# Moving a small transposition behind the convolution, in a TensorE-bound attention and feed-forward kernel

## The chip, the cores and the metric

The kernel runs on one core of one Trainium2 chip. The metric is the device time of one execution in microseconds, taken as the median of several runs. Engines are called by the profile's names: PE (TensorE, with PEld for its weight loads), DVE (VectorE), ACT (ScalarE), POOL (GpSimd), SP (SyncE, which issues most DMAs).

## The reference

The input x is 128 x 32 x 512. Cut to what matters here, the reference computes this:

```python
# per batch element: rows are mixed with weights that depend on cond
y  = einsum('boi,bih->boh', agg_w(cond), x) + agg_b(cond)
# attention: 32 query heads, 8 key/value heads, head size 16, rope, causal
x  = x + softmax(causal(q(y) @ k(y).T / 4)) @ v(y) @ Wo
# grouped convolution with 9 taps, plus a term of cond
z  = conv(x, weight, groups=4, taps=9) + ctx(cond) + bias
# feed-forward: a base product plus a low-rank part with routed experts
h  = z @ A.T                         # 8 experts x rank 16 = 128 columns
w  = routed expert weights from softmax(z @ router_W.T)
x  = x + z @ base_W.T + base_b + ((h * w) @ B) * 2
```

The kernel calls `h * w` **hw**. It is 128 tokens x 128, and has to be transposed before it can be multiplied by B ("lora").

## The kernel before, in words

**Tiling.** The 128 batch elements are taken in 32 groups (G = 32) of four, so that one group has 128 tokens and fills the 128 partitions. Products need more precision than one pass gives, so each operand is split into a high part (`_hi`, a rounded copy) and a low part (`_lo`, the value minus its high part), and a product is three matmuls: high x high, high x low, low x high.

**Software pipeline.** All engines run the same hand-written loop over t, each with its own `steps(t)`, and meet only through semaphores. Step t does the attention of group t, the projection of y into queries, keys and values for group t+1, the convolution of group t-1, and the feed-forward and lora of group t-2. Steps -1 to 3 and 31 to 33 are unrolled; steps 4 to 30 are 27 turns of a hardware loop, in which the count in a wait comes from a register. The order inside a step is that of the code, engine by engine.

**The part of PE's step that matters.** After the projection of group t+1 (L420), PE transposes the normalized softmax of group t (`transpose_p`, L642, eight matmuls into banks 2 and 4), then hw of group t-2 (`transpose_hw`, L669, into bank 7), then runs the convolution (`conv`, L623: four matmuls with 96 rows and 32 columns each, each in its own column group and recorded as two passes), then the attention's values (`values`, L662: 16 matmuls of 64 rows and 32 columns, recorded as 32 passes, into banks 4 and 7), then `lora` (L561 into bank 6, L564 into bank 2), then the output projection (`project`, L576, twelve matmuls into bank 3). In the loop, `values` first issues a tiny matmul with two columns that nobody reads (L656); it carries the last of the waits that stand ahead of the values: `vB_in` (the values' DMA), `hwT_lo_sb` (bank 7 has been read) and `pT_sb` (the transposed softmax has been copied).

**ACT.** Its step copies the first half of the transposed softmax (`transposed_p(t, 0)`), then hwT into `hwT_hi`, then the second half, then half of the attention's output into `oT_hi`, then the values of the next group into `vS` (all these copies are recorded at L755).

**DVE.** After the routing of group t-2, which ends with hw (L1130), it does the rope of the next group's queries (L1141, L1143), then `hwT_lo` (the `minus` helper, L980), then the rope of the keys (L1141, L1143 again, smaller), then `low_oT`: the other half of `oT_hi` (L1190) and `oT_lo` (L980), then the bias of the convolution (L1199) and the two output additions (L1209, L1211). `project` waits for both halves of `oT_hi`.

**DMA.** SP loads the convolution's input `xc` (recorded as scratch, L385) and the values `vB` (L355) early in each step.

Of the kernel before, what the change touches and what calls it, by code (L numbers as in the profile page):

```python
# [15 lines left out]
P = 128  # L16
B = 128
S = 32
D = 512
NB = P // S  # L20
G = B // NB
# [15 lines left out]
BASE6 = 2 * P  # L37
# [33 lines left out]
def live(u):  # L71

    return not isinstance(u, int) or 0 <= u < G


def peeled(t, n):

    return isinstance(t, int) and t == n
# [8 lines left out]
def build(nc, x, cond, fside, cW0, cb0, cW1, cb1, cW2, cb2, cweight, cbias, Wq, Wk, Wv, Wo,  # L87
          convw, convc, baseW, baseb, routerW, routerb, loraA, loraB, emap, const, out):
    with ExitStack() as ctx:
# [321 lines left out]
        def _(pe):  # L411
# [143 lines left out]
            def lora(u):  # L555

                pe.wait_ge(hwT_hi_sb, u + 1)
                pe.wait_ge(hwT_lo_sb, u + 1)
                terms = ((hwT_hi, lora_hi), (hwT_hi, lora_lo), (hwT_lo, lora_hi))
                for n, (a, b) in enumerate(terms):  # L560
                    last = mm(ps[:, 6, 0:BASE6], a[:, :], b[:, 0:BASE6], start=False, stop=(n == 2))  # L561
                last.then_inc(ffn_ps, 1)
                for n, (a, b) in enumerate(terms):
                    last = mm(ps[:, 2, 0:D - BASE6], a[:, :], b[:, BASE6:D], start=(n == 0), stop=(n == 2))  # L564
                last.then_inc(last_ps, 1)

            def project(u):

# [75 lines left out]
                    if b % 2:  # L644
                        last.then_inc(pT_ps, 1)

            def values(t):

                pe.wait_ge(vB_in, 16 * HK * (t + 1))
                if live(t - 2):  # L650
                    pe.wait_ge(hwT_lo_sb, t - 1)
                if peeled(t, 1):
                    pe.wait_ge(base_lo_sb, PH)
                pe.wait_ge(pT_sb, 2 * t + 2)
                if not isinstance(t, int):
                    mm(ps[0:S, 4, 0:2], convW[:, 0, :, :].rearrange("p j o -> p (j o)"), xc[:, 0, 0:2], start=True, stop=True)  # L656
                for b in range(NB):
                    for h in range(2):
                        for r in range(2):
                            rows = slice(2 * S * r, 2 * S * (r + 1))  # L660
                            to = S * (2 * h + (r + b) % 2)
                            last = mm(ps[to:to + S, 4 + 3 * (b % 2), b // 2 * P:(b // 2 + 1) * P],  # L662
                                      vB[rows, b, h, :], prT[rows, 2 * b + h, :], start=True, stop=True)
                last.then_inc(o_ps, 1)

            def transpose_hw(u):

                pe.wait_ge(hw_sb, u + 1)
                nc.tensor.transpose(ps[:, 7, 0:P], hw[:, :, :].rearrange("p e r -> p (e r)"), ident).then_inc(hwT_ps, 1)  # L669

            def steps(t):
                if peeled(t, 1):
                    pe.wait_ge(base_lo_sb, 2)
                if live(t):
                    transpose_qk(t)
                if peeled(t, 0):
                    prepare_ar()
                if peeled(t, 2):
                    pe.wait_ge(base_lo_sb, PH)
                if live(t - 2):  # L680
                    transpose_z(t - 2)
                if peeled(t, G + 1):
                    keep_warm(3)
                if peeled(t, -1):
                    pe.wait_ge(mixw0_sb, 1)
                if peeled(t, 3):
                    pe.wait_ge(mixw_in, 16 * NB)
                if peeled(t, 0):
                    pe.wait_ge(mixw_in2, 16 * NB)
                if live(t + 1):  # L690
                    mix(t + 1)
                if peeled(t, -1):
                    first_bias()
                    mixing_weights()
                if peeled(t, 2):
                    prepare_lora()
                if live(t):
                    scores(t)

                if peeled(t, 1):  # L700
                    prepare_base((2, 3))
                if live(t - 2):
                    feed_forward(t - 2)
                if live(t + 1):
                    queries(t + 1)
                    keys_values(t + 1)

                if peeled(t, -1):
                    prepare_conv()
                if peeled(t, 0):  # L710
                    pe.wait_ge(convW_sb, 1)
                if live(t):
                    transpose_p(t)
                if peeled(t, 0):
                    pe.wait_ge(prep_sb, 1)
                    prepare_base((0, 1))
                if peeled(t, G - 1):
                    conv(t - 1)
                if peeled(t, G):
                    pe.wait_ge(sx_sb, 2 * G)  # L720
                    keep_warm(4)
                if live(t - 2):
                    transpose_hw(t - 2)
                if peeled(t, G) or peeled(t, G + 1):
                    keep_warm(3)
                if peeled(t, G):
                    lora(t - 2)
                if live(t - 1) and not peeled(t, G - 1):
                    conv(t - 1)
                if peeled(t, G):  # L730
                    keep_warm(2)
                if live(t):
                    values(t)
                if live(t - 2) and not peeled(t, G):
                    lora(t - 2)
                if peeled(t, 0):
                    pe.wait_ge(wo_hi_sb, NQ)
                    pe.wait_ge(wo_lo_sb, NQ)
                if live(t):
                    project(t)  # L740
# [4 lines left out]
        def _(act):  # L745
# [8 lines left out]
            def copy(dst, src):  # L754
                return nc.scalar.activation(dst, src, ACT.Copy)  # L755
# [85 lines left out]
            def steps(t):  # L841
                if live(t):
                    act.wait_ge(qT_ps, t + 1)
                    copy(qT, ps[:, 4, :].rearrange("p (g b q) -> p b g q", g=NQ, b=NB)).then_inc(qT_sb, 1)
                if live(t - 2):
                    act.wait_ge(zT_ps, t - 1)
                    copy(z_hi[:, :, :].rearrange("p j (q o) -> p j q o", o=CG), z_transposed()).then_inc(z_hi_sb, 1)
                if peeled(t, 0):
                    act.wait_ge(rope_t, 2)
                    keep_values()  # L850
                    prepare_ar()
                if live(t + 1):
                    next_y_hi(t + 1)
                if peeled(t, 0):
                    prepare_wo((0, 1))
                if peeled(t, -1):
                    prepare_kv()
                    keep_mixing_weights()
                if peeled(t, 2):
                    prepare_lora()  # L860
                if live(t):
                    exponentials(t, 0)
                if live(t - 2):
                    act.wait_ge(ar_ps, t - 1)
                    copy(arS[:, :], ps[:, 7, D - BASE6:D - BASE6 + NAR]).then_inc(ar_sb, 1)
                if live(t):
                    exponentials(t, 1)
                if live(t - 2):
                    act.wait_ge(top_sb, t - 1)
                    nc.scalar.activation(ex[:, :], lg[:, :], ACT.Exp, bias=top[:, :], accum_out=exZ[:, :]).then_inc(ex_sb, 1)  # L870
                if peeled(t, 0):
                    prepare_wo((2, 3))
                if peeled(t, 1):
                    prepare_base((2, 3))

                if live(t):
                    transposed_p(t, 0)
                if live(t) and peeled(t, G - 1):
                    transposed_p(t, 1)
                if live(t - 2):  # L880
                    act.wait_ge(hwT_ps, t - 1)
                    copy(hwT_hi[:, :], ps[:, 7, 0:P]).then_inc(hwT_hi_sb, 1)
                if live(t) and not peeled(t, G - 1):
                    transposed_p(t, 1)
                if live(t):
                    act.wait_ge(o_ps, t + 1)
                    copy(heads(oT_hi, 0), heads_ps(0)).then_inc(oT_hi_sb, 1)
                if peeled(t, 0):
                    prepare_base((0, 1))
                if live(t + 1) and not peeled(t, -1):  # L890
                    act.wait_ge(rope_t, 2 * (t + 2))
                    keep_values()
# [82 lines left out]
        def _(dve):  # L975
# [237 lines left out]
            def steps(t):  # L1213
# [47 lines left out]
                    prepare_conv()  # L1261
                if live(t - 2):
                    dve.wait_ge(hwT_hi_sb, t - 1)
                    minus(hwT_lo[:, :], ps[:, 7, 0:P], hwT_hi[:, :]).then_inc(hwT_lo_sb, 1)
                if live(t + 1) and not peeled(t, -1):
                    rope(t + 1, 1, qkv_ps, D, P)
                if live(t):
# [35 lines left out]
```

## Time and profile before

| | us |
|---|---|
| median of 3 runs | 617.46 |
| the three runs | 617.46, 617.57, 613.9 |
| the profiled execution, own time | 615.38 |
| its span, first to last instruction | 613.6 |
| PE busy | 585.4 (95% of the span) |
| PEld busy | 492.8 (80%) |
| DVE busy | 494.0 (81%) |
| ACT busy | 221.4 (36%) |
| POOL busy | 226.7 (37%) |

The mean granted clock of TensorE is 0.997 of full speed. The hardware turns of the loop are alike and follow each other every 17.53 us. The profile is read in four ways here: the page's share of the chain that ended last; that chain in order of time; the timeline of single turns, whose rows give start, duration, engine, line, operation and what ended the idle time before; and the waits summed by line.

### The profile page before, as it was taken

The numbers are of one execution on the slowest core, as the hardware profiler recorded it, in microseconds if no ns is written. First come the engines' busy times: TensorE is split into PE (matmuls) and PEld (weight loads), VectorE is DVE, ScalarE is ACT, GpSimd is POOL, SyncE is SP. The second block draws the span as 40 slices with busy tenths as digits, with TensorE's granted clock in tenths as the row PEclk, the third lists the DMA queues.
The fourth block names the chain that finished last, engine by engine and source line by source line (L and its number), as shares of the span: only waits on it lengthen the run. The fifth ranks groups of instructions, "written<-read, shape, count | busy, mean of one in ns | idle before, by whom it ended". The sixth has DMA issues, their size and how long they took to land.

```text
span 613.6 us, 14243 instructions
## 1 busy us (share of the span) xinstructions
PE 585.4 (95%) x4928; PEld 492.8 (80%) x4928; DVE 494.0 (81%) x1236; ACT 221.4 (36%) x603; POOL 226.7 (37%) x182
## 2 busy tenths in 40 slices
PE   4988999999999999999999999999999999999875
PEld 4666798888888988888889888888898878888664
DVE  4677888888888888888888888888888878888843
ACT  4263334333333333333333333333333333333311
POOL 8164234433333344333333443333334333343310
PEclk9989999999999999999999999999999999999999
DMA  7844454344545543445555434454554344554430
GB/s 195 174 115 114 112 134 127 100 101 106 118 116 133 133 121 98 104 106 118 116 133 133 121 99 104 105 118 116 133 133 121 88 107 104 111 133 111 112 86 36
DMA packets 125206, 71.26 MB, mean 116 GB/s; under 512 B 48781, under 2 KB 107309, under 8 KB 125064
## 3 DMA queue, kind: packets, MB, share of 16 engines
q1 hardware_dynamic: 123696, 70.53, 48.0%
q10 hardware_dynamic: 1352, 0.27, 0.3%
q0 software_dynamic: 144, 0.28, 0.2%
q8 instruction: 8, 0.13, 0.1%
q14 instruction: 6, 0.05, 0.0%
HBM read 51.53 MB, written 19.53 MB: 116 GB/s over the span
## 4 chain that ended last, share of the span: by engine, by line
PE 83%; DVE 6%; DMA 5%; issue 2%; ACT 1%; SPq 1%; ACTq 1%; DVEq 0%
PE ps L420 19%; PE ps L576 15%; PE ps L597 10%; PE ps L603 6%; PE ps L623 5%; DMA scratch<-x_dram 5%; PE ps L524 4%; PE ps L615 4%; PE ps L642 4%; PE ps L662 3%; PE ps L561 3%; PE ps L587 2%; PE ps L631 2%; PE ps L564 2%; PE ps L611 1%
## 5 line engine op out<-in xcount | busy, mean ns | idle before, releaser
L957 POOL TENSOR_TENSOR qk<-network,t 128x640 f32<-128x640 f32 x31 | 48.3, 1560 | 161.2 <-DVE t L1143 161.2
L420 PE MATMUL ps<-wqkv_hi,y_hi 128*128 128x512 f32 (+1 forms) x256 | 88.2, 345 | 3.6 <-DVE raw L1162 2.2
L420 PE MATMUL ps<-wqkv_hi,y_lo 128*128 128x512 f32 (+1 forms) x256 | 88.3, 345 | 0.0
L420 PE MATMUL ps<-wqkv_lo,y_hi 128*128 128x512 f32 (+1 forms) x256 | 88.1, 344 | 0.0
L969 POOL TENSOR_TENSOR raw<-x1p,basebB 128x512 f32<-128x512 f32 x32 | 49.5, 1548 | 58.2 <-DVE x1p L1222 58.2
L755 ACT ACTIVATE raw<-ps 128x512 f32<-128x512 f32 x64 | 37.8, 595 | 74.3 <-PE ps L642 74.2
L964 POOL TENSOR_TENSOR raw<-raw,zero 128x512 f32<-128x512 f32 x32 | 33.3, 1041 | 72.1 <-DVE raw L1211 72.1
L420 PEld LDWEIGHTS ps<-wqkv_hi,y_hi 128*128 128x128 f32 x256 | 49.3, 192 | 11.8 <-DVE raw L1162 3.6
L941 POOL TENSOR_TENSOR raw<-raw,rz 128x512 f32<-128x512 f32 x32 | 33.7, 1052 | 56.4 <-DVE rz L1172 56.4
L420 PEld LDWEIGHTS ps<-wqkv_lo,y_hi 128*128 128x128 f32 x256 | 49.3, 193 | 6.2
L420 PEld LDWEIGHTS ps<-wqkv_hi,y_lo 128*128 128x128 f32 x256 | 49.1, 192 | 6.0
L817 ACT ACTIVATE raw<-raw 128x512 f32<-128x512 f32 x64 | 40.4, 632 | 34.0 <-DVE raw L1162 31.1
L755 ACT ACTIVATE qk_t<-ps 128x512 f32<-128x512 f32 x32 | 19.1, 597 | 91.6 <-PE ps L587 91.6
L597 PE MATMUL ps<-ffn_hi,z_hi 128*128 128x400 f32 x128 | 46.9, 366 | 2.3 <-DVE z_lo L980 2.3
L947 POOL TENSOR_TENSOR y_lo<-ys,y_hi 128x512 fp32r<-128x512 f32 x31 | 40.4, 1305 | 21.0 <-ACT y_hi L755 21.0
L1151 DVE TENSOR_TENSOR qk_t<-ps,cst 128x512 f32<-128x512 f32 x32 | 22.1, 691 | 32.2 <-PE ps L585 32.1
L1160 DVE TENSOR_REDUCE mx<-ps 128x16 f32<-128x512 f32 x64 | 43.9, 686 | 2.7 <-PE ps L615 0.4
L1162 DVE TENSOR_TENSOR raw<-ps,mx 128x512 f32<-128x512 f32 x64 | 44.3, 692 | 2.2
L597 PE MATMUL ps<-ffn_lo,z_hi 128*128 128x400 f32 x128 | 44.4, 346 | 0.0
L597 PE MATMUL ps<-ffn_hi,z_lo 128*128 128x400 f32 x128 | 44.0, 344 | 0.0
L1170 DVE TENSOR_REDUCE sm<-raw 128x16 f32<-128x512 f32 x64 | 41.8, 653 | 0.0
L755 ACT ACTIVATE vS<-ps 32x64 f32<-32x64 f32 (+1 forms) x192 | 37.5, 226 | 1.1
(185 smaller groups left out, 1459.9 us busy)
## 6 DMA issues: line engine op xcount, KB each, us to landing
scratch<-x_dram SPq DMA_DIRECT2D x96, 256.0 KB, 5.8
x_dram<-x1p SPq DMA_DIRECT2D x32, 260.0 KB, 2.1
xm<-x SPq DMA_DIRECT2D x32, 256.0 KB, 4.4
xr<-x SPq DMA_DIRECT2D x32, 256.0 KB, 2.7
out<-raw SPq DMA_DIRECT2D x32, 256.0 KB, 2.0
v_dram<-vS SPq DMA_DIRECT2D x32, 64.0 KB
vB<-v_dram SPq DMA_DIRECT2D x128, 16.0 KB, 4.9
mixb<-mixb_dram SPq DMA_DIRECT2D x28, 64.0 KB, 3.8
```

The lines of the kernel that those rows point to most:

```text
L420: last = mm(dst, a, b, start=(n == 0), stop=(n == 3 * len(left) - 1))
L576: last = mm(ps[:, 3, :], a[:, g, :, :].rearrange("p b q -> p (b q)"), b[:, g, :], start=(n == 0 and g == 0), stop=(n == 2 and g == NQ - 1))
L597: last = mm(ps[:, 7, 0:D - BASE6 + NAR], a, b[:, BASE6:D + NAR], start=(n == 0), stop=(n == len(terms) - 1))
L603: mm(ps[:, 6, 0:BASE6], a, b[:, 0:BASE6], start=(n == 0), stop=False)
L755: return nc.scalar.activation(dst, src, ACT.Copy)
L817: nc.scalar.activation(pr[:, D * h:D * (h + 1)], sx[:, D * h:D * (h + 1)], ACT.Exp, scale=HD ** -0.5).then_inc(p_sb, 1)
L947: nc.gpsimd.tensor_tensor(y_lo[:, :], ys[:, :], y_hi[:, :].bitcast(F32), ALU.subtract).then_inc(y_lo_sb, 1)
L957: nc.gpsimd.tensor_tensor(qk[:, :], t1, t2[:, :], ALU.add).then_inc(qk_sb, 1)
L969: nc.gpsimd.tensor_tensor(x1c, x1, basebB[:, :].rearrange("p (n j) -> p j n", j=PH), ALU.add).then_inc(x1c_sb, 1)
L1160: v.tensor_reduce(m, s3, AX.X, ALU.max).then_inc(mx_sb, 1)
L1162: v.tensor_tensor(sx[:, D * h:D * h + D].rearrange("p (h m) -> p h m", m=S), s3, m.unsqueeze(2).broadcast_to([P, 16, S]), ALU.subtract).th ...
L1170: v.tensor_reduce(sm[:, m], p3, AX.X, ALU.add).then_inc(sm_sb, 1)
```

## The change

On PE, the transposition of hw moves from ahead of the convolution to behind it, and writes bank 3 instead of bank 7. The waits that stood ahead of the values, without that for `hwT_lo_sb`, now stand ahead of this transposition (`values_ready`), and the unread product is gone. In `lora`, the four matmuls with `hwT_hi` come first, and the wait for `hwT_lo_sb` stands ahead of the last two. On ACT, both halves of the transposed softmax are copied ahead of `hwT_hi`. On DVE only the bank that is read changes. Steps 31 to 33 keep their order, since the convolution was ahead of the transposition in step 31 already, and step 32 keeps its transposition and lora ahead of the convolution; they take over the new waits and the new order inside `lora`.

```diff
             def lora(u):
                 pe.wait_ge(hwT_hi_sb, u + 1)
+                for n, right in enumerate((lora_hi, lora_lo)):
+                    mm(ps[:, 6, 0:BASE6], hwT_hi[:, :], right[:, 0:BASE6], start=False, stop=False)
+                for n, right in enumerate((lora_hi, lora_lo)):
+                    mm(ps[:, 2, 0:D - BASE6], hwT_hi[:, :], right[:, BASE6:D], start=(n == 0), stop=False)
                 pe.wait_ge(hwT_lo_sb, u + 1)
-                terms = ((hwT_hi, lora_hi), (hwT_hi, lora_lo), (hwT_lo, lora_hi))
-                for n, (a, b) in enumerate(terms):
-                    last = mm(ps[:, 6, 0:BASE6], a[:, :], b[:, 0:BASE6], start=False, stop=(n == 2))
-                last.then_inc(ffn_ps, 1)
-                for n, (a, b) in enumerate(terms):
-                    last = mm(ps[:, 2, 0:D - BASE6], a[:, :], b[:, BASE6:D], start=(n == 0), stop=(n == 2))
-                last.then_inc(last_ps, 1)
+                mm(ps[:, 6, 0:BASE6], hwT_lo[:, :], lora_hi[:, 0:BASE6], start=False, stop=True).then_inc(ffn_ps, 1)
+                mm(ps[:, 2, 0:D - BASE6], hwT_lo[:, :], lora_hi[:, BASE6:D], start=False, stop=True).then_inc(last_ps, 1)
...
-            def values(t):
+            def values_ready(t):
                 pe.wait_ge(vB_in, 16 * HK * (t + 1))
-                if live(t - 2):
-                    pe.wait_ge(hwT_lo_sb, t - 1)
                 if peeled(t, 1):
                     pe.wait_ge(base_lo_sb, PH)
                 pe.wait_ge(pT_sb, 2 * t + 2)
-                if not isinstance(t, int):
-                    mm(ps[0:S, 4, 0:2], convW[:, 0, :, :].rearrange("p j o -> p (j o)"), xc[:, 0, 0:2], start=True, stop=True)
+
+            def values(t):
+                if not live(t - 2):
+                    values_ready(t)
...
             def transpose_hw(u):
                 pe.wait_ge(hw_sb, u + 1)
-                nc.tensor.transpose(ps[:, 7, 0:P], hw[:, :, :].rearrange("p e r -> p (e r)"), ident).then_inc(hwT_ps, 1)
+                if live(u + 2):
+                    values_ready(u + 2)
+                nc.tensor.transpose(ps[:, 3, 0:P], hw[:, :, :].rearrange("p e r -> p (e r)"), ident).then_inc(hwT_ps, 1)
...
-                if peeled(t, G - 1):
-                    conv(t - 1)
                 if peeled(t, G):
                     pe.wait_ge(sx_sb, 2 * G)
                     keep_warm(4)
-                if live(t - 2):
                     transpose_hw(t - 2)
-                if peeled(t, G) or peeled(t, G + 1):
                     keep_warm(3)
-                if peeled(t, G):
                     lora(t - 2)
-                if live(t - 1) and not peeled(t, G - 1):
+                if live(t - 1):
                     conv(t - 1)
+                if live(t - 2) and not peeled(t, G):
+                    transpose_hw(t - 2)
+                if peeled(t, G + 1):
+                    keep_warm(3)
...
                 if live(t):
                     transposed_p(t, 0)
-                if live(t) and peeled(t, G - 1):
                     transposed_p(t, 1)
                 if live(t - 2):
                     act.wait_ge(hwT_ps, t - 1)
-                    copy(hwT_hi[:, :], ps[:, 7, 0:P]).then_inc(hwT_hi_sb, 1)
-                if live(t) and not peeled(t, G - 1):
-                    transposed_p(t, 1)
+                    copy(hwT_hi[:, :], ps[:, 3, 0:P]).then_inc(hwT_hi_sb, 1)
...
                     dve.wait_ge(hwT_hi_sb, t - 1)
-                    minus(hwT_lo[:, :], ps[:, 7, 0:P], hwT_hi[:, :]).then_inc(hwT_lo_sb, 1)
+                    minus(hwT_lo[:, :], ps[:, 3, 0:P], hwT_hi[:, :]).then_inc(hwT_lo_sb, 1)
```

On PE, in the body of the loop, this is the order before, from the transposed softmax (`ps<-cst,raw`) over hw, the convolution (`scratch,convW`), the unread product (32x2) and the values (`raw,vB`) to lora:

```order
L642 MATMUL ps<-cst,raw 128x128 x7
L669 MATMUL ps<-cst,hw 128x128 [waits hw_sb]
L621 REGISTER_ALU
L623 MATMUL ps<-scratch,convW 32x512 [waits xc_in]
L623 MATMUL ps<-scratch,convW 32x512 x3
L649 REGISTER_ALU
L654 REGISTER_ALU [waits hwT_lo_sb,vB_in]
L656 MATMUL ps<-scratch,convW 32x2 [waits pT_sb]
L662 MATMUL ps<-raw,vB 32x128 x16
L561 MATMUL ps<-lora_hi,hwT_hi 128x256 [waits hwT_lo_sb,hwT_hi_sb]
L561 MATMUL ps<-lora_lo,hwT_hi 128x256
L561 MATMUL ps<-lora_hi,hwT_lo 128x256
```

And this is the same place after the change:

```order
L641 MATMUL ps<-cst,raw 128x128 x7
L620 REGISTER_ALU
L622 MATMUL ps<-scratch,convW 32x512 [waits xc_in]
L622 MATMUL ps<-scratch,convW 32x512 x3
L648 REGISTER_ALU [waits hw_sb]
L651 REGISTER_ALU [waits vB_in]
L671 MATMUL ps<-cst,hw 128x128 [waits pT_sb]
L662 MATMUL ps<-raw,vB 32x128 x16
L559 MATMUL ps<-lora_hi,hwT_hi 128x256 [waits hwT_hi_sb]
L559 MATMUL ps<-lora_lo,hwT_hi 128x256
L561 MATMUL ps<-lora_hi,hwT_hi 128x256
L561 MATMUL ps<-lora_lo,hwT_hi 128x256
```

The transposition of hw has taken the place of the unread product, and the values wait for nothing of their own.

On DVE the order is the same in both kernels. This is its part of the loop from hw to the output's first addition, of the kernel before (`network` and `t` are the rope's two buffers):

```order
L1130 SCALAR_TENSOR_TENSOR hw<-arS,exR,we 128x128 [waits we_sb]
L1141 TENSOR_TENSOR network<-ps,cst 128x512 [waits qk_sb,q_ps]
L1143 TENSOR_TENSOR t<-ps,cst 128x32x8 x2
L980 TENSOR_TENSOR hwT_lo<-ps,hwT_hi 128x128 [waits hwT_hi_sb]
L1141 TENSOR_TENSOR network<-ps,cst 128x128 [waits qk_sb,qkv_ps]
L1143 TENSOR_TENSOR t<-ps,cst 128x8x8 x2
L1190 CAST oT_hi<-ps 128x8x32 [waits o_ps]
L980 TENSOR_TENSOR oT_lo<-ps,oT_hi 128x8x32 [waits oT_hi_sb]
```

Nothing moved here: the wait for `hwT_hi_sb` still stands ahead of the rope of the keys and of `oT_hi`.

## Rows read from the trace of the kernel before

**Rows 1.** The page: busy times, and the chain that ended last by engine

```profile
PE 585.4 (95%) x4928; PEld 492.8 (80%) x4928; DVE 494.0 (81%) x1236; ACT 221.4 (36%) x603; POOL 226.7 (37%) x182
...
PE 83%; DVE 6%; DMA 5%; issue 2%; ACT 1%; SPq 1%; ACTq 1%; DVEq 0%
```

**Rows 2.** The chain in order of time, one turn: start, us, what

```profile
302.46 0.11 PE ps L669
302.57 1.00 PE ps L623 x8
303.57 0.16 PE ps L656 x2
```

**Rows 3.** Timeline of one turn of the loop, PE: start, us, engine, line, operation

```profile
302.30 0.27 PE L669 MATMUL ps<-cst,hw 128*128 128x128 f32 x1
302.50 0.16 PEld L623 LDWEIGHTS ps<-scratch,convW 96*32 96x32 f32 x8 [0.17 <-DMA scratch<-x_dram]
...
303.50 0.14 PEld L656 LDWEIGHTS ps<-scratch,convW 96*32 96x32 f32 x2 [0.85 <-ACT raw L755]
...
303.66 0.67 PE L662 MATMUL ps<-raw,vB 64*32 64x128 f32 x32
...
304.26 0.39 PE L561 MATMUL ps<-lora_hi,hwT_hi 128*128 128x256 f32 x1
...
305.06 1.10 PE L576 MATMUL ps<-wo_hi,oT_hi 128*128 128x512 f32 x4
```

**Rows 4.** Timeline of the same turn, ACT and DVE

```profile
302.61 0.28 ACT L755 ACTIVATE hwT_hi<-ps 128x128 fp32r<-128x128 f32 x1
302.78 0.59 ACT L755 ACTIVATE raw<-ps 128x512 f32<-128x512 f32 x1
302.99 0.28 DVE L980 TENSOR_TENSOR hwT_lo<-ps,hwT_hi 128x128 fp32r<-128x128 f32 x1
...
303.38 0.35 DVE L1143 TENSOR_TENSOR t<-ps,cst 128x64 f32<-128x64 f32 x2
...
304.43 0.42 DVE L1190 CAST oT_hi<-ps 128x256 fp32r<-128x256 f32 x1 [0.70 <-PE ps L662]
```

**Rows 5.** Timeline, two turns in which the convolution's input came late

```profile
250.01 0.16 PEld L623 LDWEIGHTS ps<-scratch,convW 96*32 96x32 f32 x8 [0.28 <-DMA scratch<-x_dram]
...
496.40 0.16 PEld L623 LDWEIGHTS ps<-scratch,convW 96*32 96x32 f32 x8 [1.20 <-DMA scratch<-x_dram]
...
497.20 0.20 PEld L656 LDWEIGHTS ps<-scratch,convW 96*32 96x32 f32 x2 [0.64 <-issue]
497.42 0.40 PEld L662 LDWEIGHTS ps<-raw,vB 64*32 64x32 f32 x32
```

**Rows 6.** Timeline of step 31, where hw is already transposed behind the convolution

```profile
583.24 0.33 PE L669 MATMUL ps<-cst,hw 128*128 128x128 f32 x1
583.61 0.28 ACT L755 ACTIVATE hwT_hi<-ps 128x128 fp32r<-128x128 f32 x1 [1.41 <-PE ps L669]
583.92 0.29 DVE L980 TENSOR_TENSOR hwT_lo<-ps,hwT_hi 128x128 fp32r<-128x128 f32 x1 [0.73 <-ACT hwT_hi L755]
584.28 0.43 PEld L662 LDWEIGHTS ps<-raw,vB 64*32 64x32 f32 x32 [0.90 <-issue]
...
585.73 1.09 PE L576 MATMUL ps<-wo_hi,oT_hi 128*128 128x512 f32 x4
```

**Rows 7.** Timeline of step 32, from the convolution to a full-array product

```profile
598.44 0.16 PEld L623 LDWEIGHTS ps<-scratch,convW 96*32 96x32 f32 x8
...
599.44 0.30 PEld L468 LDWEIGHTS ps<-wo_hi 128*128 128x128 f32 x2 [0.84 <-issue]
```

**Rows 8.** Timeline of step 2: hw, the convolution, and the output projection

```profile
74.32 0.14 PEld L669 LDWEIGHTS ps<-cst,hw 128*128 128x128 f32 x1 [0.89 <-DVE hw L1130]
...
74.58 0.16 PEld L623 LDWEIGHTS ps<-scratch,convW 96*32 96x32 f32 x8
...
77.26 1.09 PE L576 MATMUL ps<-wo_hi,oT_hi 128*128 128x512 f32 x4
```

## The prediction

> **What bounds the kernel now.** I read the page first. PE is busy for 95% of the span, and the chain that ended last lies on PE for 83% [rows 1]. Then I read that chain in order of time: inside the loop it never leaves PE. One turn goes from hw's transposition (0.11 us) and the convolution (1.00) straight to the unread product (0.16) [rows 2], and from there over the values (303.66 to 304.26) into lora [rows 3]. So whatever shortens PE's row by a tenth of a microsecond in each of the 27 turns gives 2.7 us, and whatever makes PE wait costs as much. Third, the timeline of one turn shows what PE waits for at the place of the change. The weights of the unread product were loaded at 303.50, after ACT's second softmax copy had ended at 302.78 + 0.59 = 303.37 [rows 3, 4]: 0.13 from ACT's end to PE's start. The convolution, which began at 302.50, was over at that moment too, so PE hardly stood still. The output projection started at 305.06, right behind lora; its other input, DVE's half of oT_hi, was ready at 304.43 + 0.42 = 304.85 [rows 3, 4]. So DVE had only 0.21 us in hand. That is the number to watch.
>
> **The convolution moves forward.** In that turn hw's transposition began at 302.30 and the convolution at 302.50 [rows 3]: 0.20 from a full-array product to the convolution. hw's own share of PE's row was 0.11 [rows 2], so with hw gone from this place the convolution starts at about 302.39, if its input is there. In 21 of the 27 turns the input did not delay it; in six it did, by a few hundredths to one microsecond; two of them are shown [rows 5].
>
> **hw's transposition behind the convolution.** It uses the full array. Step 32 shows what that costs: the convolution began at 598.44 and the next full-array weights at 599.44, with nothing to wait for and 0.84 us of idle loader ahead [rows 7]. So hw's weights load 1.00 us after the convolution's start, at 303.39. The unread product had it easier: with the convolution's own shape, its weights went in 0.80 us after a late convolution's start (497.20 against 496.40), and the values followed 1.02 us after it [rows 5]. From hw's weights to the next tiled product it is 0.26 us (74.32 to 74.58) [rows 8], so the values start at 303.39 + 0.26 = 303.65, where they started at 303.66. Neither of the moved waits is late: the second softmax copy no longer has hwT_hi ahead of it, which took 302.61 to 302.78, so it ends at 303.20 and releases PE at 303.33; hw itself has been ready since before the old place. The product that goes saves 0.16, the moved one saves 0.11 at its old place and costs 0.26 at its new one: PE's own row gains 0.01.
>
> The Trainium skill (TensorEngine Tiling, Key Properties) says that a change of tiling mode, not just of tile, drains the engine. By that rule the change adds one such change per turn, full array between two tiled products, and the trace agrees with its 0.84 us of idle loader.
>
> **The new wait on DVE.** What hangs on hw now starts a microsecond later. Step 31 has this order already. There ACT's hwT_hi started 0.37 after hw's product, and DVE's hwT_lo 0.31 after that [rows 6]. From 303.39 this gives hwT_hi at 303.76 to 304.04 and hwT_lo at 304.07 to 304.36; in the turn shown hwT_lo started at 302.99 [rows 4]. DVE takes its work in order, and behind hwT_lo stand the rope of the keys and then oT_hi. The rope ended 0.74 after hwT_lo's start (303.38 + 0.35 against 302.99) [rows 4]; a DVE instruction that has nothing to wait for starts up to 0.09 before the end of the one ahead, so oT_hi starts 0.66 to 0.74 after hwT_lo. I take 0.66, since this is how the rows of the rope follow each other. So oT_hi starts at 304.73, not 304.43, and ends at 305.15. From DVE's end to PE it was 0.07 in step 31 (584.21 to 584.28) [rows 6]; the projection has one more wait, I take 0.08. It starts at 305.23, not 305.06: **0.17 us later**. Ends: 0.10 if the overlap and the release are a little better; 0.28 if the convolution's input, which is not seen to land early, never lets it start before 302.50.
>
> Lora is not the one that is late: it starts at 303.65 + 0.60 = 304.25, when hwT_hi has been there for 0.2 us, comes to its low part at about 304.84, when hwT_lo has been there for 0.5 us, and has issued its six products at 305.05. Its new order hides nothing that was open in the loop; at its old order it would have had hwT_lo in time too. Behind the waiting projection are only PE's own later products, and by the timeline DVE and POOL have room there.
>
> **The sum over the loop.** In each turn the projection now starts 1.00 + 0.37 + 0.31 + 0.66 + 0.42 + 0.08 = 2.84 us after the convolution. Before, it was 305.06 - 302.50 = 2.56. With a convolution 0.11 earlier this is +0.17, times 21 turns = +3.6. In the six turns with a late input nothing moves forward, and the slack of up to 0.15 that the short product left is lost too: +0.28 to +0.43 each, three near each end by how late they were, together +2.3. Loop: **+5.9 us**.
>
> **Outside the loop.** Step 3 had no unread product: it loses 0.17 and the 0.16 that it never spent, some 0.3. In step 2, hw came late and held the convolution: 0.89 us of idle loader ahead of hw [rows 8]. Now the convolution can start 0.17 after the softmax weights, at 73.60, and the projection 2.84 later, at 76.44, not 77.26. This is -0.82 if its input is there, and +0.16 if it comes as late as 74.58; no row tells, I take -0.6. In step 31 the values no longer wait for hwT_lo: they start 0.26 after hw, at 583.50, not 584.28, lora follows and the projection starts at 584.90, not 585.73 [rows 6]: -0.8. In steps 32 and 33 lora's high part goes ahead of the wait for hwT_lo; the last product comes 0.3 earlier in step 32, and at the very end DVE's addition waits for one product after the low part, not three: -0.05. Together -1.4.
>
> **Total:** +5.9 - 1.4 = +4.5 us, 0.7%. The profiled execution took 615.4, the median of the runs shown is 617.5. I start half way, from 616.4, and come to **620.9**.
>
> **Rivals.**
> (A) *The full-array weights slip under the convolution.* If hw's weights can be loaded while the convolution still streams, as those of the unread product were [rows 5], its product starts some 0.15 earlier and the chain over DVE with it: the projection is where it was, +0.02 a turn; the loop costs about 1, the ends give 1.4: 616.0, not slower. Against it stands the idle loader of step 32 [rows 7].
> The Trainium skill (TensorE: Matmul & The Clock Gate, Architectural detail) says that PE can pull weight loads ahead of matmuls in flight. By that rule this case would be the one; step 32 does not show it.
> (B) *PE alone decides.* If besides that DVE's chain had its slack back (the rope's rows closer than I read them), the PE row would lose 0.15 a turn: -4 in the loop, -1.4 outside: 611.0. It needs oT_hi 0.15 earlier than rows 4 and 6 give, and I see nothing for it.
> (C) *The convolution's input sets the start in every turn.* The wait ahead of the convolution is put down to this DMA even in the turn shown, where it cost nothing [rows 3]. If it lands just at the old start, moving hw away gives nothing: 21 x 0.28 + 2.3 = 8.2 in the loop, -0.6 outside: 624.0, slower. It decides once the input lands after 302.39 in this turn's time.
> (D) *DVE becomes the bound.* It is busy for 81% [rows 1] and would stand still for 1 us more per turn, but it idled 0.70 at oT_hi [rows 4] and has idle time behind it. It decides if the late hwT_lo costs DVE 0.4 us a turn or more: 10.8 - 1.4, or 626.
>
> **How the numbers follow.** My forecast 0.55, A 0.14, B 0.05, C 0.18, D 0.08. The range that holds 8 in 10 runs from 614.0 (A with its spread) to 626.0 (C, and D's edge). One percent, 6.2 us, is about what a measurement of this kernel can tell from no change. Faster by over 1%: what is in B, 0.06. Slower by over 1%: C, D and the upper edge of the forecast, 0.30. Within 1%: 0.64.
>
> **What would show it.** In the new profile: the chain in order of time leaves PE in each turn, over hwT_hi, hwT_lo and oT_hi, ahead of the projection; a wait of the projection for DVE's oT_hi (L1188 or near), 0.1 to 0.2 us in all 27 turns; hw's weights 1.00 us after the convolution's; a period of 17.7 us instead of 17.53; DVE idle ahead of hwT_lo for about 1 us. I would be wrong in the step on the drain if hw's weights load under 0.95 us after the convolution's start, in the step on DVE if the projection follows lora without a gap, and in both if the period is below 17.53.

## The result, and the profile after

| | before | after |
|---|---|---|
| median | 616.48 us (4 runs, 613.9 to 617.57) | 623.32 us (4 runs, 620.9 to 624.0) |
| ratio | | 1.0117, 95% interval 1.008 to 1.0154 |
| profiled execution, own time | 615.38 | 623.83 |
| its span | 613.6 | 622.0 |

The change made the kernel 1.2% slower. The forecast was 620.9, 0.7% slower, with a range from 614.0 to 626.0.

The page of the changed kernel shows nearly the same busy shares as [rows 1]; the share of DMA in the chain that ended last has doubled, and that of PE has fallen:

```profile
PE 592.7 (95%) x4874; PEld 491.9 (79%) x4874; DVE 491.6 (79%) x1236; ACT 225.9 (36%) x603; POOL 226.3 (36%) x182
...
PE 76%; DMA 11%; DVE 5%; SPq 3%; issue 2%; ACT 1%; ACTq 1%; DVEq 0%
```

That share is no measure of the loss: it is 10% in the rope-first run below, which is as fast as the kernel before, and 1% in the changed kernel with an earlier input, which is nearly as slow as this one.

This is the chain of the changed kernel in order of time over one turn of the loop (start, us, what), which answers to [rows 2]:

```profile
307.14 1.00 PE ps L622 x8
308.13 0.26 PE ps L671
308.39 0.60 PE ps L662 x32
308.99 0.43 PE ps L559 x2
309.42 0.24 PE ps L561 x2
309.66 0.12 PE ps L563
309.77 0.12 PE ps L564
309.89 0.03 issue
309.92 3.04 PE ps L575 x12
```

hw's transposition (L671) takes 0.26 us behind the convolution. Near the bottom there are 0.03 us of "issue": in this turn, this small row is all that the chain sets apart from PE's own work. The projection's row has 3.04 us where the kernel before and the first experiment below have 2.81, but only a part of that is slower work. In the timeline the projection takes 2.88 us from its own start to that of the next product (309.92 to 312.80), against 2.81 in both others; the other 0.16 us is waiting that the chain has booked as projection (the last product of lora starts at 309.61, and these follow each other every 0.12, so with the 0.03 the wait is 0.19). The chain names DVE nowhere in this turn: a reader who looks only for engine names there will miss the wait.

The timeline of the same turn is what [rows 3, 4] were before:

```profile
307.06 0.16 PEld L622 LDWEIGHTS ps<-scratch,convW 96*32 96x32 f32 x8 [0.17 <-DMA scratch<-x_dram]
...
308.06 0.14 PEld L671 LDWEIGHTS ps<-cst,hw 128*128 128x128 f32 x1 [0.84 <-ACT raw L756]
...
308.32 0.67 PE L662 MATMUL ps<-raw,vB 64*32 64x128 f32 x32
308.43 0.28 ACT L756 ACTIVATE hwT_hi<-ps 128x128 fp32r<-128x128 f32 x1 [0.60 <-PE ps L671]
308.74 0.29 DVE L978 TENSOR_TENSOR hwT_lo<-ps,hwT_hi 128x128 fp32r<-128x128 f32 x1 [1.00 <-ACT hwT_hi L756]
...
309.14 0.34 DVE L1141 TENSOR_TENSOR t<-ps,cst 128x64 f32<-128x64 f32 x2
...
309.40 0.41 DVE L1188 CAST oT_hi<-ps 128x256 fp32r<-128x256 f32 x1
...
309.89 0.76 PEld L575 LDWEIGHTS ps<-wo_hi,oT_hi 128*128 128x128 f32 x4 [0.20 <-issue]
309.92 1.16 PE L575 MATMUL ps<-wo_hi,oT_hi 128*128 128x512 f32 x4
```

Read from the convolution's start: hw's weights at +1.00, the values at +1.26, hwT_hi at +1.37, hwT_lo at +1.68, oT_hi at +2.34, the projection at +2.86. The projection was at +2.56 before. DVE's oT_hi has no idle time ahead of it any more, where it idled 0.70 in [rows 4]; the idle time has moved up, ahead of hwT_lo (1.00). The loader of the projection stood still for 0.20 us. The profile puts that down to "issue", because DVE's oT_hi ended only 0.08 us before (309.40 + 0.41 = 309.81); it is the wait for DVE all the same, as the first experiment shows.

One line of the waits summed by line (total us, times, longest) has all turns of it:

```profile
PEld ps L575 <- issue: 6.8, 30, 1.0
```

The regular turns follow each other every 17.78 us, not every 17.53. Eight turns of the loop had a late convolution input, with 2.9 us of idle loader beyond the usual 0.17; in the profile of before it was six turns with 1.9 us.

**Where the 8.4 us of span are.** The convolution of step 4 starts at 110.38 instead of 109.62: +0.8. From there to the one of step 30 there are 26 periods, which take 465.4 us instead of 457.3: +8.1, of which 26 x 0.25 = 6.5 is in the regular turn and 1.6 in the turns with a late input. The rest of the program is 0.5 shorter. Medians of several runs differ by less, 6.8 us. Each profile is a single execution, and executions of one kernel differ: in their late inputs, and in where the granted clock falls (the last section). How much of the gap between 8.4 and 6.8 is due to either is not shown. The clock is not the cause of the loss: the changed kernel's only execution at a mean granted clock of 1.000 took 620.9 us, and the kernel before took 613.5 to 613.7 us in its four at that clock.

### The profile page after: what moved, and what is told of

Same layout as the page of the kernel before. It is cut to its first block, busy times and chain, and to the rows that moved or that the text cites. A ratio compares the mean times of both kernels' runs of the same rounds, so it can differ in the third digit from the quotient of the medians.

```text
span 622.0 us, 14076 instructions
## 1 busy us (share of the span) xinstructions
PE 592.7 (95%) x4874; PEld 491.9 (79%) x4874; DVE 491.6 (79%) x1236; ACT 225.9 (36%) x603; POOL 226.3 (36%) x182
## 4 chain that ended last, share of the span: by engine, by line
PE 76%; DMA 11%; DVE 5%; SPq 3%; issue 2%; ACT 1%; ACTq 1%; DVEq 0%
PE ps L420 16%; PE ps L575 16%; DMA scratch<-x_dram 10%; PE ps L596 9%; PE ps L622 5%; PE ps L602 5%; PE ps L524 3%; PE ps L614 3%; PE ps L662 3%; PE ps L641 3%; PE ps L559 2%; DVE x1p L1220 2%; PE ps L586 2%; PE ps L630 2%; PE ps L671 1%
## 5 line engine op out<-in xcount | busy, mean ns | idle before, releaser
L756 ACT ACTIVATE raw<-ps 128x512 f32<-128x512 f32 x64 | 34.7, 595 | 74.2 <-PE ps L641 74.1
L575 PE MATMUL ps<-wo_hi,oT_hi 128*128 128x512 f32 x128 | 37.3, 413 | 2.2 <-DVE oT_hi L1188 0.7
```

Of the source, the lines that this page charges most:

```text
L575: last = mm(ps[:, 3, :], a[:, g, :, :].rearrange("p b q -> p (b q)"), b[:, g, :], start=(n == 0 and g == 0), stop=(n == 2 and g == NQ - 1))
```

## The experiments

All ratios are against the kernel before, run on the same chip between the others.

### The rope of the keys ahead of hwT_lo

The edit, on DVE in the changed kernel:

```diff
-                if live(t - 2):
-                    dve.wait_ge(hwT_hi_sb, t - 1)
-                    minus(hwT_lo[:, :], ps[:, 3, 0:P], hwT_hi[:, :]).then_inc(hwT_lo_sb, 1)
                 if live(t + 1) and not peeled(t, -1):
                     rope(t + 1, 1, qkv_ps, D, P)
+                if live(t - 2):
+                    dve.wait_ge(hwT_hi_sb, t - 1)
+                    minus(hwT_lo[:, :], ps[:, 3, 0:P], hwT_hi[:, :]).then_inc(hwT_lo_sb, 1)
```

> The changed kernel, but on DVE the rope of the keys stands ahead of hwT_lo, so that DVE's half of oT_hi no longer waits behind the rope behind hwT_lo. If the loss comes from that queue on DVE, the projection follows lora without a gap, 2.66 us after the convolution's start instead of 2.86, its first four matmuls take 1.10 us again instead of 1.16, the period falls from 17.78 to about 17.53, and the time to about 616.5 us. If the loss comes from the extra full-array product between two tiled ones, or from the convolution's input, nothing changes: 622 to 624 us.

Measured: 614.62 us, ratio 0.998 (0.9964 to 0.9996). The regular period is 17.53 (17.52 and 17.53 by turns). The timeline of one turn:

```profile
304.83 0.33 PE L671 MATMUL ps<-cst,hw 128*128 128x128 f32 x1
...
305.51 0.29 DVE L978 TENSOR_TENSOR hwT_lo<-ps,hwT_hi 128x128 fp32r<-128x128 f32 x1 [0.53 <-ACT hwT_hi L756]
...
305.87 0.42 DVE L1188 CAST oT_hi<-ps 128x256 fp32r<-128x256 f32 x1
...
306.50 1.09 PE L575 MATMUL ps<-wo_hi,oT_hi 128*128 128x512 f32 x4
```

oT_hi now starts 1.04 us after hw's product instead of 1.34, and the projection 1.67 after it instead of 1.86, without a gap behind lora and with 1.09 instead of 1.16 for its first four matmuls. The line "PEld ps L575 <- issue" shrank from 6.8 us in 30 turns to 1.0 us in one. hwT_lo still starts 0.68 us after hw's product, as in the changed kernel: the rope of the keys now fills time in which DVE idled. Moving these instructions on DVE took back all that the change had lost: the loss was the queue on DVE. The extra change between full array and tiles is still in this kernel and does not make it slower than before.

### The bank alone

The kernel before, with hw transposed into bank 3, where it stood, and without the values' wait for hwT_lo:

```diff
-                nc.tensor.transpose(ps[:, 7, 0:P], hw[:, :, :].rearrange("p e r -> p (e r)"), ident).then_inc(hwT_ps, 1)
+                nc.tensor.transpose(ps[:, 3, 0:P], hw[:, :, :].rearrange("p e r -> p (e r)"), ident).then_inc(hwT_ps, 1)
...
-                if live(t - 2):
-                    pe.wait_ge(hwT_lo_sb, t - 1)
```

> The kernel before with the bank alone changed: hw is transposed at its old place, but into bank 3, and the values no longer wait for hwT_lo; the unread product stays. All theories: that wait was never the last one in the loop, so the loop is as before (period 17.53); step 31 and step 2 gain up to 0.8 us each where the values did wait for it. 614.5 to 616.5 us, within 0.3% of before. If the bank itself costs something, it is slower.

Measured: 612.9 us, ratio 0.9956 (0.9932 to 0.9981): more than expected. The regular period is 17.46, not 17.53. The wait that I had called "never the last" cost 0.07 us a turn. The timeline shows where, the ends of ACT's copy and the unread product (L654 here):

```profile
300.81 0.59 ACT L753 ACTIVATE raw<-ps 128x512 f32<-128x512 f32 x1
...
301.45 0.14 PEld L654 LDWEIGHTS ps<-scratch,convW 96*32 96x32 f32 x2 [0.77 <-ACT raw L753]
```

Only 0.05 us lie between them, where [rows 3, 4] have 0.13. Two more runs went after this.

### One more wait, long satisfied

To the bank-3 kernel one wait was added, on hw:

```diff
                 pe.wait_ge(vB_in, 16 * HK * (t + 1))
+                if live(t - 2):
+                    pe.wait_ge(hw_sb, t - 1)
```

> The bank-3 run with one more wait on PE ahead of the unread product, against a register and on hw_sb, which has been satisfied long before. In the bank-3 run the period fell from 17.53 to 17.46 when the wait for hwT_lo went, though that was never the last to be satisfied. If PE's issue of a wait costs that time, the period is 17.53 again; if hwT_lo's semaphore itself did it, it stays 17.46. 612 to 616 us.

Measured: 613.47 us, ratio 0.996 (0.9939 to 0.9982), most periods 17.46. An extra wait in the same place costs nothing here; it was the wait for hwT_lo in particular.

### ACT's new order with the old bank

The kernel before with only this edit on ACT (the wait for hwT_lo ahead of the values stays):

```diff
-                if live(t) and peeled(t, G - 1):
-                    transposed_p(t, 1)
+                if live(t):
+                    transposed_p(t, 1)
                 if live(t - 2):
                     act.wait_ge(hwT_ps, t - 1)
                     copy(hwT_hi[:, :], ps[:, 7, 0:P]).then_inc(hwT_hi_sb, 1)
-                if live(t) and not peeled(t, G - 1):
-                    transposed_p(t, 1)
```

> The kernel before with only ACT's order changed: both softmax copies ahead of hwT_hi, hw still in bank 7 and the values still waiting for hwT_lo. hwT_lo then ends some 1.14 us after the convolution's start, clearly last. In the kernel before it ended 0.77 us after it, and the unread product started 0.23 us after that. If a wait for hwT_lo in the middle of the three takes 0.23 us from DVE's end to PE, the unread product's weights load 1.37 us after the convolution's start and the period is 17.90; if it takes the usual 0.07 to 0.13, 1.21 to 1.27 us and 17.74 to 17.80. 620 to 628 us either way: this is what bank 7 costs with ACT's new order.

Measured: 624.7 us in a single execution, beside 616.13 for one of the kernel before; the reading rests on the regular turns, which are alike. The timeline:

```profile
306.88 0.16 PEld L623 LDWEIGHTS ps<-scratch,convW 96*32 96x32 f32 x8 [0.17 <-issue]
...
307.73 0.29 DVE L978 TENSOR_TENSOR hwT_lo<-ps,hwT_hi 128x128 fp32r<-128x128 f32 x1 [0.27 <-ACT hwT_hi L755]
...
308.26 0.14 PEld L656 LDWEIGHTS ps<-scratch,convW 96*32 96x32 f32 x2 [1.22 <-ACT raw L755]
```

The unread product's weights load 1.38 us after the convolution's start and 0.24 after hwT_lo's end; the next convolution starts 17.91 after this one. This is the first of the two cases, to 0.01 us. The profile's own label is wrong: ACT's copy had ended 0.7 us earlier. In the kernel before, hwT_lo ended at 302.99 + 0.28 = 303.27 and the unread product came at 303.50 [rows 3, 4], the same 0.23. So hwT_lo, not ACT, released the unread product there. Why this wait, the second of three, takes 0.23 us from DVE to PE, when step 31 had 0.07 [rows 6], was not tried; the last section says what the traces add.

### Both softmax copies first, hw ahead of the convolution

The bank-3 kernel with ACT's new order (the edit above, with bank 3). The unread product stays.

> The kernel before with bank 3 (as in e3) and both softmax copies ahead of hwT_hi on ACT; hw stays ahead of the convolution, the unread product stays. The second copy ends 0.17 us earlier, so the unread product's weights load while the convolution still streams, as they did in turns with a late input, and the values start 1.01 us after the convolution, not 1.16. hwT_lo is then 0.46 us later than before and still leaves oT_hi in time. Period 17.38 instead of 17.53, time 610 to 612.5 us, 0.7% faster than before. If the unread product costs its 0.16 us wherever it stands, nothing changes: 615 to 616.5 us.

Measured: 610.26 us, ratio 0.9934 (0.9911 to 0.9956). The regular period is 17.39. The timeline of one turn:

```profile
299.53 0.16 PEld L623 LDWEIGHTS ps<-scratch,convW 96*32 96x32 f32 x8 [0.17 <-issue]
...
300.23 0.30 PEld L654 LDWEIGHTS ps<-scratch,convW 96*32 96x32 f32 x2 [0.54 <-ACT raw L753]
...
300.54 0.67 PE L660 MATMUL ps<-raw,vB 64*32 64x128 f32 x32
...
301.32 0.42 DVE L1186 CAST oT_hi<-ps 128x256 fp32r<-128x256 f32 x1 [0.18 <-PE ps L660]
...
301.95 1.09 PE L576 MATMUL ps<-wo_hi,oT_hi 128*128 128x512 f32 x4
```

The unread product's weights load 0.70 us into the convolution, and the values follow 1.01 us after its start: the product costs nothing when its waits are early. The projection comes at +2.42. So the unread product, which the change removed, was not the cost; its late wait was. Against the rope-first run, which has hw behind the convolution and PE bound as well, the period is 0.14 shorter: that is the price on PE of hw's new place (0.26 there, 0.11 saved at the old one).

The regular periods of these runs take the change apart. Without the wait for hwT_lo the turn is 0.07 us shorter (17.53 to 17.46), and ACT's new order takes another 0.07 (17.39). hw's new place costs 0.14 (17.53, the rope-first run), and the queue on DVE 0.25 (17.78). If the parts add, as they do here to 0.01 us, two gains and a loss cancel, and what remains is the queue.

### Lora in its old order

The changed kernel with lora as it was, both waits ahead of its six matmuls.

> The changed kernel with lora's matmuls in their old order, both waits ahead. If DVE's oT_hi sets the projection's start, lora starts some 0.2 us later and ends just when the projection could start anyway: 622.5 to 625 us, at most 0.1 us a turn more. If PE's own row set it, each turn would be 0.2 us longer: 628 us or more.

Measured: 622.96 us, ratio 1.0115 (1.0081 to 1.0148); regular periods 17.77 to 17.80. As expected, lora's order does nearly nothing while DVE holds the projection. But it is not idle, as I had said. Three rows of one turn, from the convolution at 305.88:

```profile
307.56 0.29 DVE L979 TENSOR_TENSOR hwT_lo<-ps,hwT_hi 128x128 fp32r<-128x128 f32 x1 [0.98 <-ACT hwT_hi L757]
...
307.99 0.36 PE L561 MATMUL ps<-lora_hi,hwT_hi 128*128 128x256 f32 x1 [0.19 <-DVE hwT_lo L979]
...
308.78 1.13 PE L576 MATMUL ps<-wo_hi,oT_hi 128*128 128x512 f32 x4
```

Lora starts at +2.11 instead of +1.86 and ends where the projection could start anyway (+2.90, against +2.86). The other half of the test was the ACT-order kernel with the change's lora:

> The kernel of the ACT-order run (hw ahead of the convolution, bank 3, both softmax copies first) with lora's high part ahead of the wait for hwT_lo, the other half of the change. In the loop hwT_lo ends 0.5 us before lora starts, so nothing changes there (period 17.39); the last two steps gain 0.3 us together. 609.5 to 611 us.

Measured: 609.95 us, ratio 0.9899 (0.9871 to 0.9927); period 17.39 as without it. The median is 0.3 us under the run without it. Those two were taken on different occasions, and the intervals of their ratios meet, so the small gain at the end is not shown.

### The convolution's input issued earlier

On SP in the changed kernel:

```diff
-                if live(t + 2) and not peeled(t, 0):
-                    sp.wait_ge(y_ps, t + 2)
-                    sp.dma_start(xm[:, :], group(x_g, t + 2)).then_inc(xm_in, 16)
                 if live(t - 1):
                     sp.wait_ge(x1_out, 16 * t)
...
+                if live(t + 2) and not peeled(t, 0):
+                    sp.wait_ge(y_ps, t + 2)
+                    sp.dma_start(xm[:, :], group(x_g, t + 2)).then_inc(xm_in, 16)
```

> The changed kernel, but SP issues the loads of the convolution's input (xc) ahead of the load of xm. If the late inputs of some turns matter (8 turns of the loop in the profile of the changed kernel, 2.9 us of idle loader beyond the usual 0.17, and step 2), and the place in SP's queue decides, up to 3 us go: 620 to 621.5 us, with the regular period still 17.78. If the queue on DVE is all, or the lateness comes from the transfers themselves, 622 to 624 us.

Measured: 620.81 us, ratio 1.0086 (1.0053 to 1.0119). The median time to landing fell from 5.8 to 4.7 us, every turn of the loop is regular (17.78 to 17.83), and the profiled span is 617.1. The loop is 2.6 us shorter than in the profile of the changed kernel (462.8 us for the 26 periods, not 465.4). The two issue groups of this transfer, in the changed kernel and then in this one:

```profile
scratch<-x_dram SPq DMA_DIRECT2D x96, 256.0 KB, 5.8
```

```profile
scratch<-x_dram SPq DMA_DIRECT2D x96, 256.0 KB, 4.7
```

The same edit in the kernel before:

> The kernel before with only SP's order changed (xc's loads ahead of xm's). Six turns of its profile had a late input, 1.9 us beyond the usual gap. If that goes as it did in the changed kernel: 613.5 to 615.5 us, ratio 0.996 to 0.999, all periods 17.53. Then the changed kernel's own loss, with late inputs out of both, is 27 turns of 0.25 us, some 1.1%. If instead late inputs were a cost of the change alone, the ratio here is 1.000.

Measured: 614.27 us, ratio 0.9966 (0.9951 to 0.9982), and every turn from step 5 on at 17.52 to 17.54. By the medians late inputs cost the kernel before about 2 us too; the loop of its profile shows 1.3 (457.3 us for the 26 periods, 456.0 here). With them out of both kernels the change still costs 1.0086 / 0.9966 = 1.012, and the two loops differ by 6.8 us, 26 times 0.26. Late inputs are not its cause.

### All of it together

The ACT-order kernel with the change's lora and the earlier input:

> The same with xc issued ahead of xm on SP. If SP's queue makes the input late, up to 2 us less than the run before it (608.5 us); if not, the same time.

Measured: 608.64 us, ratio 0.9901 (0.9866 to 0.9936), and every turn from step 5 on at 17.38 or 17.39. It beats the kernel before by 1.0%, and the changed one, dividing the two ratios, by 2.1% (0.9901 / 1.0117). Against the run without the earlier input (0.9899) the ratio does not tell a gain.

## Why the prediction was right, and where it was off

**The convolution moves forward, hw behind it: right.** hw's weights load 1.00 us after the convolution's start in all turns of the loop, and the values 0.26 later. The drain held, so rival A fell: the full-array weights never slipped under the convolution, with an idle loader of 0.84 us as in [rows 7]. PE's own row was to gain 0.01 a turn; the rope-first run, in which DVE holds nothing up, has the period of the kernel before within 0.01.

**What bounds PE there before: misread.** I put the unread product's start down to ACT's copy, by the profile's label and 0.13 us of distance. The old-bank run shows that hwT_lo set it, at a cost of 0.07 us a turn. The prediction's sum was not touched, since it measured the old turn from its own rows.

**The new wait on DVE: right, and a little small.** The offsets of hwT_hi (+0.37), hwT_lo (+0.31) and oT_hi (+0.66) from step 31 and the rope held to 0.01 us. The step "0.42 + 0.08" measured 0.52, so the projection came at +2.86, not +2.84. And one term was missing: I let the projection start late but run on as before. Where nothing holds it, its first weights load 0.12 us ahead of its first product (304.94 and 305.06 in the kernel before); behind the wait they were only 0.03 ahead (309.89 and 309.92), and its first four matmuls took 1.16 us, not 1.10. This is the row of the kernel before:

```profile
304.94 0.78 PEld L576 LDWEIGHTS ps<-wo_hi,oT_hi 128*128 128x128 f32 x4
```

Together the regular turn costs 0.25, not 0.17, over 27 turns 6.8 instead of 4.6: this is the largest miss of the sum.

**Lora: wrong in a side remark.** "At its old order it would have had hwT_lo in time too" did not hold. The forecast's own times said so: hwT_lo was to end at 304.36, and lora to start at 304.25. Measured, the old order starts lora 0.25 us later. That moved the projection's start by 0.04 and the period hardly at all, because DVE held the projection anyway.

**Outside the loop.** Step 31 gained what was said: from convolution to projection 3.69 us before [rows 6], 2.95 now (-0.8 forecast, -0.7 measured). In step 32 the distance from hw to the convolution fell by 0.35 (-0.3 forecast). Step 2 failed: I took -0.6 although no row told when its input lands. It landed after the old start:

```profile
74.80 0.16 PEld L622 LDWEIGHTS ps<-scratch,convW 96*32 96x32 f32 x8 [1.66 <-DMA scratch<-x_dram]
```

With the convolution at 74.80 the projection came at 77.65, not 76.44: 0.4 later than before [rows 8]. That is the bound that I had given for the late case (+0.16, with the convolution at 74.58) and another 0.2 for an input that landed later still.

**The sum against the two profiles.** From the convolution of step 4 to that of step 31 the 27 turns cost +8.4 us, forecast +5.9. Of the 2.5 missing, 2.2 are the regular turn. The rest is in the turns with a late input: 1.6 us beyond the regular cost, where the sum had 1.3; its term of 2.3 for six such turns should read 2.1 by its own bounds (three at 0.28, three at 0.43). Ahead of the loop it was +0.8, forecast -0.3; behind it -0.7, forecast -1.1, with the last stretch at the lower clock. So the spans of the two profiles lie 3.9 us further apart than forecast, and all three misses point the same way; that the median came within 2.4 us of 620.9 is in part the draw of the executions.

**The rivals.** C had its part but is not the cause: the input was late in eight turns, not in every one, and taking lateness out of both kernels leaves the ratio at 1.012. D fell: DVE is less busy by share than before, and the period returns as soon as two of its instructions change places. B fell with A.

**How it was to show.** The period was to be 17.7 and is 17.78. The chain was to leave PE in each turn; it does not, it shows 0.03 us of "issue", and the waits show "issue" too. The sign I named was wrong though the wait was there. DVE's idle time ahead of hwT_lo was to be about 1 us and is 1.00.

## What to carry to other kernels

When a product moves down on one engine, follow every instruction that stands behind its consumers on the other engines: here a 0.29 us subtraction on DVE carried its wait into the output of the attention, which had 0.21 us in hand. A cheap instruction that only carries waits is not a cost by itself; look at which of its waits ends last, and do not trust the label of a wait when several stand there: change one at a time. And when PE is made to wait even briefly, add what it loses because its weights are no longer loaded ahead (0.06 us a turn here).

## What the runs showed of the hardware that was not expected

A wait for hwT_lo between two others took 0.23 to 0.24 us from DVE's end to PE's next weights, in the kernel before and in the run that made it clearly last; a spare, long satisfied wait in its place cost nothing. Elsewhere a wait for the same semaphore was shorter: 0.07 us in the unrolled steps 2 and 31 of the kernel before, which have no unread product, and 0.11 us ahead of lora in the loop of the run with lora in its old order (hwT_lo ended at 307.85, lora's weights loaded at 307.96). So neither the semaphore nor the loop makes it long by itself; what does stays open.

TensorE's granted clock fell late in some executions. The last lora of the changed kernel's profile ran slower for it. Here are three stretches around it; the columns are the stretch, the busy us (with counts) of PE, PEld, DVE, ACT and POOL, the granted clock, the DMA share and GB/s:

```profile
612.00:616.00 4.00, 2.38 (x18) 2.17 (x16) 1.94 (x11) 0.69 (x3) 0.00 (x0) 1.00 0.01 2
616.00:617.00 1.00, 0.65 (x4) 0.55 (x4) 0.29 (x1) 0.28 (x1) 0.00 (x0) 1.00 0.00 0
617.00:618.60 1.60, 1.60 (x8) 1.30 (x6) 0.43 (x2) 0.00 (x0) 0.00 (x0) 0.58 0.00 0
```

The granted clock fell from 1.00 (2.4 GHz) to a mean of 0.58, so to the lower level (1.2 GHz) for most of the last 1.6 us, after stretches in which PE was busy for 2.38 of 4.00 us and 0.65 of 1.00. From the load of the last hw to the end of the span it was 5.63 us, 5.26 before, although lora itself started 0.26 us sooner behind hw.

A longer fall stands in step 31 of other profiles, here the run of the bank alone (the same columns):

```profile
570.00:577.00 7.00, 5.38 (x46) 5.05 (x44) 6.12 (x13) 1.96 (x6) 2.59 (x2) 1.00 0.84 194
577.00:578.00 1.00, 0.48 (x8) 0.24 (x10) 0.92 (x6) 1.00 (x2) 0.00 (x0) 0.82 0.32 39
578.00:584.00 6.00, 6.00 (x51) 3.44 (x52) 3.86 (x11) 0.74 (x3) 0.00 (x0) 0.50 0.00 0
```

For these 6 us the clock was at the lower level, 1.2 GHz. The profiles of three more runs (rope first, spare wait, lora in its old order) show the same, and in these four 18.1 to 18.4 us lie between the convolutions of steps 31 and 32. It was 15.3 in the profile of the changed kernel and 16.4 in that of the kernel before, where the clock stayed at 1.00 in this place. So a single time can be 2 to 3 us longer for it, an estimate from these distances. Over the 63 executions of the kernel before that stand beside the experiments, the median was 614.8 us for those with a mean granted clock of 0.997 and 616.2 for those with 0.992. This is why the readings above rest on the period of the regular turns, which ran at a clock of 1.00 in every profile, and use the medians beside it.
